# Two transformer blocks over eight batches: a work order of its own for each engine, a fetch in two parts, and stack loads of 256 KB

## What is computed

```python
xn = _layernorm(x)
x = x + _L0_attn_ref(xn, ...) + _L0_ffn_ref(xn, ...)     # block 0
xn = _layernorm(x)
x = x + _L1_attn_ref(xn, ...) + _L1_ffn_ref(xn, ...)     # block 1
```

## Time and profile before

| | us |
|---|---|
| median of 3 runs | 795.38 |
| lowest and highest | 793.43, 795.67 |
| the profiled execution, whole | 790.95 |
| its span | 789.2 |

### The profile page before, as it was taken

The page is one execution under the profiler, slowest core; times in us unless marked ns, Lnnn a source line. Parts: engine busy times, 40 slices in busy tenths (PEclk is TensorE's granted clock), DMA queues, the critical chain, the costliest instruction groups (busy, mean ns, idle before and its releaser), DMA issues. The chain is left out here.

```text
span 789.2 us, 19922 instructions
## 1 busy us (share of the span) xinstructions
PE 654.3 (83%) x6455; PEld 481.4 (61%) x6455; DVE 568.9 (72%) x2201; ACT 465.8 (59%) x1223; POOL 267.8 (34%) x386
## 2 busy tenths in 40 slices
PE   0466677999699997999799997999699997899834
PEld 0344455777477765777577765777477776677512
DVE  3679877786579757786679757786679768776464
ACT  2458765955388445955388445955388447944433
POOL 7926441233213331223213331323213332134334
PEclk9969797999999998999999998999989999999969
DMA  7643021301211031301211031301211030300552
GB/s 219 231 132 99 23 72 50 105 19 55 84 54 55 15 109 29 108 15 55 83 54 55 15 109 29 108 15 55 83 54 55 15 108 15 108 2 15 165 182 69
DMA packets 49580, 57.69 MB, mean 73 GB/s; under 512 B 5056, under 2 KB 40000, under 8 KB 49472
## 3 DMA queue, kind: packets, MB, share of 16 engines
q1 hardware_dynamic: 46432, 52.44, 20.8%
q0 software_dynamic: 1056, 2.62, 1.0%
q10 hardware_dynamic: 1984, 1.21, 0.6%
HBM read 33.71 MB, written 22.54 MB: 71 GB/s over the span
## 5 line engine op out<-in xcount | busy, mean ns | idle before, releaser
L1001 ACT ACTIVATE probs<-probs,nmax 128x256 f32<-128x256 f32 (+1 forms) x256 | 113.5, 446 | 51.4 <-DVE nmax L1511 50.5
L844 POOL TENSOR_TENSOR h_lo<-hid,h_hi 128x512 f16<-128x512 f32 x64 | 74.2, 1160 | 203.5 <-ACT h_hi L982 203.3
L1125 PE MATMUL gen_ps<-xe_hi,gu_hi 128*128 128x256 f16 x512 | 101.6, 281 | 3.2 <-DVE gated L1457 2.0
L1125 PE MATMUL gen_ps<-xe_lo,gu_hi 128*128 128x256 f16 x512 | 100.7, 279 | 0.0
L1125 PE MATMUL gen_ps<-xe_hi,gu_lo 128*128 128x256 f16 x512 | 100.4, 279 | 0.0
L1029 ACT ACTIVATE et<-turn_ps 128x384 f32<-128x384 f32 x128 | 55.7, 489 | 66.1 <-PE turn_ps L1215 56.1
L1511 DVE CUSTOM_DVE_ANT_0 probs<-score_ps,bias 128x256 f32<-128x256 f32 (+1 forms) x256 | 80.2, 352 | 19.0 <-PE score_ps L1182 11.2
L1525 DVE CUSTOM_DVE_ANT_0 junk<-score_ps,bias 128x256 bf16<-128x256 f32 (+1 forms) x256 | 76.0, 352 | 16.2 <-PE score_ps L1182 11.3
L1180 PE MATMUL score_ps<-k_stack,q_stack 64*128 64x256 f16 x256 | 37.9, 292 | 51.5 <-DVE nmax L1511 17.9
L1536 DVE TENSOR_SCALAR probs<-probs,rsum 128x256 f32<-128x256 f32 (+1 forms) x256 | 74.6, 334 | 4.5
L1473 DVE SCALAR_TENSOR_TENSOR acc<-gen_ps,w,acc 128x256 f32<-128x256 f32 x112 | 48.8, 477 | 25.5 <-PE gen_ps L1136 25.4
(11 more groups left out here) (210 smaller groups left out, 1664.5 us busy)
## 6 DMA issues: line engine op xcount, KB each, us to landing
scr_q<-parts SPq DMA_DIRECT2D x32, 256.0 KB, 2.7
scr_k<-parts SPq DMA_DIRECT2D x32, 256.0 KB, 3.0
q_stack<-scr_q SPq DMA_DIRECT2D x64, 128.0 KB, 3.0
k_stack<-scr_k SPq DMA_DIRECT2D x64, 128.0 KB, 3.1
x<-in_x SPq DMA_DIRECT2D x8, 256.0 KB, 3.5
y_dram<-yx_sb SPq DMA_DIRECT2D x7, 256.0 KB, 2.2
x_dram<-yx_sb SPq DMA_DIRECT2D x7, 256.0 KB, 2.3
gu_hi<-y_dram SPq DMA_DIRECT2D x1, 1792.0 KB, 7.7
```

The costliest lines, as they stand in the source:

```text
L844: pool.tensor_tensor(h0_lo[:, e], hid0[:, e], h0_hi[:, e], ALU.subtract).then_inc(s_h0l, 1)
L1001: last = act.activation(probs[:, k, lo:hi], probs[:, k, lo:hi], ACT.Exp, scale=-1.0, bias=nmax[:, k, j:j + 1], accum_out=esum[:, k, j:j + 1])
L1125: last = pe.matmul(g[:, S * f:S * f + S], w[:, st.arg, m, k, cols], xx[:, k, :], start=(i == 0), stop=(i == len(terms) - 1))
```

## The change

- The texts, `with_heads` and `LAG` go. In their place stands `ORDER_TEXT`, with a list of single steps for each of PE, ACT, DVE and POOL in each pass; each engine's list holds only the steps in which it has work. SP goes on taking PE's list.
- `load_stack` issues one load of 256 KB (128 rows) for q and one for k, in place of two of 128 KB each; PE's wait counts 32 for a stack, not 64.
- `fetch` has two parts: part 0 brings batches 0 to 5 and waits for the stores of these only, part 1 brings batch 6 and waits for its store. ACT and POOL wait for part 0 at `quant:0` and for part 1 at `quant:6`. In SP's list part 1 stands behind the output stores of `quant:0` and `quant:1`.
- The first reduction of `qmax` (over the y maxima) becomes a step of its own, `ymx`.

The number of compute instructions of each kind, their shapes and the semaphores are otherwise the same.

```diff
-                for hp in range(2):
-                    four = slice(8 * u + 4 * hp, 8 * u + 4 * hp + 4)
-                    for src, dst in zip(scr[l], (q_stack, k_stack)):
-                        sp.dma_start(dst[l][u][KR * hp:KR * hp + KR],
-                                     src.rearrange("s (c h) n -> (s c) h n", h=H)[:, four, :]).then_inc(s_stack[l][u], 16)
+                for src, dst in zip(scr[l], (q_stack, k_stack)):
+                    by_head = src.rearrange("s (c u p i) n -> u p (s c) (i n)", u=2, p=2, i=H // 4)
+                    sp.dma_start(dst[l][u][:].rearrange("r i n -> r (i n)"), by_head[u]).then_inc(s_stack[l][u], 16)
...
+                    c = st.arg
                     sp.wait_ge(s_acc, NT * ACC_STEPS * B)
-                    sp.wait_ge(s_yw, 16 * B)
-                    sp.wait_ge(s_x2w, 16 * B)
-                    done = NT * (B - 1)
-                    sp.dma_start(y_all[:, 0:done, :], y_tiles[:, 0:done, :]).then_inc(s_fin, 16)
-                    sp.dma_start(x_all[:, 0:done, :], x2_tiles[:, 0:done, :]).then_inc(s_fin, 16)
+                    sp.wait_ge(s_yw, 16 * (EARLY + 1 if c == 0 else B))
+                    sp.wait_ge(s_x2w, 16 * (EARLY + 1 if c == 0 else B))
+                    part = slice(0, NT * EARLY) if c == 0 else slice(NT * EARLY, NT * (B - 1))
+                    sp.dma_start(y_all[:, part, :], y_tiles[:, part, :]).then_inc(s_fin[c], 16)
+                    sp.dma_start(x_all[:, part, :], x2_tiles[:, part, :]).then_inc(s_fin[c], 16)
...
-                    if c == 0:
-                        pool.wait_ge(s_fin, 32)
+                    if c in (0, EARLY):
+                        pool.wait_ge(s_fin[c // EARLY], 32)
```

More of the change, by code:

```diff
@@ L128, in in_turn @@
     return [next(turns[key(item)[0]]) for item in items]
[L131 to L137, removed]
-            out.append(("score", s, 0))
-        if 0 <= s - NORM_LAG < H:
-            out.append(("norm", s - NORM_LAG, 0))
-        t = s - TURN_LAG
-        if 0 <= t < H:
-            out.append(("turn", t, 0))
-        t -= VALUE_LAG
-        if 0 <= t < H and t % G4 == G4 - 1:
-            out.append(("value", t // G4, 0))
-    for item in order:
-        if isinstance(item, int):
-            head(item)
-        else:
-            out.append(item)
-    return out
@@ L156 @@
-FIRST_ORDER = """
-    ln0a setup:0 ln0b split:0 split:3 tr0 setup:2 xe split:2 vsplit:0 split:1 v0:0 q0 k0 gate:0 setup:1 l0 split:5 rt1
-    v0:1 split:4 up:0 gate:1 0 rt2 split:7 1 up:1 split:6 down:0 2 gate:2 3 down:1 4 up:2 split:8 gate:3 5 split:9
-    up:3 down:2 tern:0 split:10 6 tmx:0 tern:1 gate:4 7 down:3 8 split:11 9 up:4 10 11 12 gate:5 tern:3 down:4 13
-    tern:2 split:13 +ln0a tern:4 up:5 tsm:0 tern:6 split:12 tern:5 gate:6 14 gate:7 +ln0b up:6 down:5 15 16 tmx:1 up:7
-    vsplit:1 +tr0 17 down:6 tern:8 tern:7 +q0 +k0 tern:9 +v0:0 +l0 18 19 +v0:1 down:7 op0 +xe tsm:1 tern:10 tern:11
@@ L162 @@
-"""
-STEADY_ORDER = """
-    0 1 ln1a gate:0 2 ln1b up:0 rt1 tr1 3 rt2 4 q1 k1 5 gate:1 down:0 6 up:1 gate:2 w1:3 w1:0 l1 w1:2 w1:1 v1 7 8 h1:0
-    up:2 9 gate:3 10 h1:1 down:1 11 h1:2 b:1 h1:3 up:3 12 down:2 13 14 down:3 15 b:0 16 gate:4 17 b:3 mp:0 up:4 +ln0a
-    mp:1 18 b:2 w2 b:4 19 m:0 gate:5 s:1 b:5 down:4 +ln0b op0 s:0 b:6 +tr0 up:5 b:7 s:2 gate:6 +q0 +k0 s:3 y:0 +l0
-    up:6 m:1 gate:7 s:4 y:1 s:5 up:7 down:5 s:6 y:2 s:7 +v0:0 down:6 y:3 down:7 +v0:1 op1 +xe
-"""
-LAST_ORDER = """
-    ln1a 0 gate:0 ln1b rt1 rt2 1 tr1 2 gate:1 up:0 3 q1 k1 4 down:0 5 up:1 6 gate:2 v1 h1:1 w1:2 w1:1 w1:0 l1 w1:3
-    up:2 7 8 down:1 9 gate:3 10 down:2 11 12 h1:3 h1:0 13 b:0 up:3 14 15 h1:2 b:1 gate:4 16 up:4 b:4 17 18 gate:5 b:3
-    down:4 mp:0 19 b:2 m:0 up:5 down:3 b:5 gate:6 up:6 gate:7 up:7 s:2 b:6 down:5 op0 s:0 mp:1 b:7 down:7 down:6 s:1
-    +ln1a y:0 s:3 m:1 +ln1b w2 +tr1 s:4 y:1 +q1 +l1 +k1 s:5 s:6 y:2 s:7 +w1:0 +w1:2 y:3 +w1:1 +w1:3 op1
@@ L182, in order_of @@
+BLOCK1 = {"b", "mp", "m", "s", "y", "ln1a", "ln1b", "tr1", "q1", "k1", "l1", "v1", "w1", "h1", "w2", "op1", "ymx", "qmax", "quant", "fetch"}
 def order_of(text):
@@ L204, in uses @@
     return sum(s[0] in BANKED for s in order)
-ORDERS = {"first": order_of(FIRST_ORDER), "steady": order_of(STEADY_ORDER),
-          "last": order_of(LAST_ORDER), "final": order_of(FINAL_ORDER)}
+ORDER_OF = {engine: {kind: order_of(text) for kind, text in kinds.items()} for engine, kinds in ORDER_TEXT.items()}
+ORDERS = ORDER_OF["tensor"]
 USES_STEADY = uses(ORDERS["steady"])
@@ L217 @@
 ACC_STEPS = E + 1
+EARLY = B - 2
 class Index:
@@ L290, in stages @@
         out.append(st)
-    def behind(st):
-        for key in (f"{kind}.{st.name}:{st.arg}", f"{kind}.{st.name}", f"{st.name}:{st.arg}", st.name):
-            if key in lag:
-                return lag[key]
-        return 0
-    late = [i + behind(st) for i, st in enumerate(out)]
-    return in_turn([out[i] for i in sorted(range(len(out)), key=lambda i: (late[i], i))],
-                   lambda st: (st.name, st.n.off, st.arg))
+    if engine not in ORDER_OF:
+        return out
+    by_step = dict(zip(ORDERS[kind], out))
+    return [by_step[step] for step in ORDER_OF[engine][kind]]
 def last_users(kind, it):
@@ L306, in last_users @@
     if kind != "first":
-        stages("last" if kind == "final" else "steady", it.plus(-1), {}, users)
+        stages("last" if kind == "final" else "steady", it.plus(-1), "", users)
     return users
@@ L331, in settle, with run_passes @@
     eng.sem_inc(passed, 1)
-def run_passes(eng, do, before_block1, lag):
-    for st in stages("first", Index(None, 0), lag):
+def run_passes(eng, do, before_block1, engine):
+    for st in stages("first", Index(None, 0), engine):
         do(st)
@@ L339, in run_passes @@
     with eng.Fori(0, STEADY) as j:
-        for st in stages("steady", Index(j, 1), lag):
+        for st in stages("steady", Index(j, 1), engine):
             do(st)
-    for st in stages("last", Index(None, B - 1), lag):
+    for st in stages("last", Index(None, B - 1), engine):
         do(st)
-    for st in stages("final", Index(None, B), lag):
+    for st in stages("final", Index(None, B), engine):
         do(st)
@@ L720, in _ @@
             load_raw(1)
-            for st in stages("first", Index(None, 0), {}):
+            for st in stages("first", Index(None, 0), "sync"):
                 if st.name == "ln0a" and st.n.off == 1:
@@ L729, in _ @@
                 load_x(it.plus(1))
-                for st in stages("steady", it, {}):
+                for st in stages("steady", it, "sync"):
                     do(st)
-            for st in stages("last", Index(None, B - 1), {}):
+            for st in stages("last", Index(None, B - 1), "sync"):
                 do(st)
-            for st in stages("final", Index(None, B), {}):
+            for st in stages("final", Index(None, B), "sync"):
                 do(st)
```

149 lines of the change are left out of this document (126 added, 23 removed), and 41 rows, old and new, of the table LAG.

## The result

The changed kernel takes 863.86 us (median of 4 runs, 863.63 to 864.01), the kernel before 795.52 (4 runs). The ratio is 1.0864, 95% interval 1.0845 to 1.0884: slower by 8.6%, where I had forecast 782.8 us. The profiled execution has a span of 862.0 us, against 789.2.

The account below looks back on a forecast made before the run. PE was taken to bound the steady iteration, DVE to be nearest full in the first pass, the end to be a chain. Gains 3.7 + 4.5 + 0 + 4.4 = 12.6 us from the 795.38 median gave 782.8 us, range 771 to 794.

Parts of the forecast that it names:

- the landing of the 256 KB load: First pass: a merged load lands in 3.2 us, and two fewer issues bring the first score 1.2 us earlier.
- In the steady passes the stacks are loaded several us before they are used, so there the saving is 0.: Steady iterations: the merged loads save 0; if the cover went, at most 1.2 us for a stack.
- The queue: SP, first pass: eight issues of about 0.60 us each; halving them brings the weight loads behind them 2.4 us earlier.
- late next: Final pass: the scale, at about 756.5, holds quant:0, which starts 2.1 us earlier, not 3.6.
- First pass: First pass: l0 1.3 us earlier from the lists, 2.4 from fewer issues; 3.7 us carried to its end.
- Steady: Six steady iterations: q1 starts 0.75 us earlier in each by the new order, 4.5 us in all.
- my fourth case: Rival, chance 0.11: without the wait at tr1 the clock holds, 3.1 us more in some four iterations, 770.4 us.
- an iteration is over 89 us: Steady loop: sign that the forecast is wrong; iterations of 87.7 us were expected against 88.5.
- Last pass: Last pass, up to op1 of batch 6: gain 0, between 1.5 us either way.
- Final pass: Final pass: 4.4 us gained from the split fetch and new order, bounds 1 and 6.
- Part (c): Final pass order: fewer quants ahead of s:0, b:6 and b:7 bring ACT's s:3 4.4 us earlier.
- The slow rival: Steady iterations, chance 0.11: the half-speed clock stretch of 6.3 us doubles, costing 3.15 us an iteration, 801.7 us.

Follow-up runs that it names:

- the kernel with two loads: Changed kernel with the stack loads as before, two of 128 KB for q and two for k: 776.59 us, ratio 0.9784; run again 779.21 us, 0.9849.
- The four passes timed alone: Old loads, new lists in one pass only (the final one with the split fetch), against the kernel before: ratios first 0.9907, steady 0.9857, last 0.9970, final 0.9952.

## Why the prediction was wrong

**The step that failed: the landing of the 256 KB load.** I bounded it "between the 3.0 us of 128 KB and that plus the transfer of another 128 KB", 0.4 us by the rate of the fetch, and took 3.2. The stack is whole 12.7 us behind its first issue, where it took 5.2 before and where I counted on 4.0 (1.2 less). The error isn't in the number but in what I scaled: bytes, at a rate that the fetch had on all engines. I had the diff with `u p (s c) (i n)` before me and read it only for which bytes it brings. The shape was a fact of the change, and neither my bounds nor a rival had it. It was also the one change in my sum for which no row of before stood. What the runs showed in its place: the load runs on 2 engines, not 16, and brings some 50 GB/s where the old loads brought 199.

**"In the steady passes the stacks are loaded several us before they are used, so there the saving is 0."** This was wrong for the kernel before too. At `b:0` PE takes its first score 5.4 us behind the first issue, and a stack takes 5.2: the cover is 0.2 us, if the 5.2 of the first pass hold here. I bounded what is lost if that cover goes with the same 1.2 us for a stack, a bound for a saving, not for a loss. It became a wait of 7.3 to 8.0 us in each iteration, 45.4 in six. Against the same lists with loads on all engines (520.9 us) the six iterations are 53.6 us longer; 4.7 of the other 8.2 are a wait at a first score, and for the rest I can name the lower clock but haven't measured it apart. Had I looked up who uses the stack and when, I'd have seen that a longer load would be paid in full, six times.

**The queue.** I counted what an issue costs SP (0.60 us) as fixed. With a narrow load it is 0.5 to 8.1 us. It looks as if SP stands at the issue until loads ahead have drained; what it stands for the profile doesn't show. All that is queued on SP behind it comes late too: the weight loads, the store of x, the fetch. That is how the end lost 16.0 us, where I had a gain of 4.4. The scale, "late next" in my text, was ready at 823.6, 6 us before the fetch. My 10.7 us for part 0 (12.49 x 6/7) took the queue ahead of it as free; the part took 17.82.

**The list terms.** In the kernel with two loads they can be held against my steps.
- First pass: l0 at 25.6 us against 26.5 walked, score:0 at 37.49 with both loads still there, where I had 37.8 with the merged one. The pass gives 4.7 us, not 1.3 without the loads. My walk on ACT was right to within 1 us; the 2.83 us that I left for l0 was 1.22, and I didn't follow what DVE and the splits gain behind l0.
- Steady: the gain is 8.6 us, not 4.5, and only a third of it came as I had it. Cut at the loop's first matmul on PE, the four iterations between the loop's turns take 87.8 us with the new lists and 88.5 with the old ones (means of four kernels each): 0.7 an iteration, where I had 0.75. But that is 2.8 us and not 4.5; the other 5.8 lie at the two ends of the loop, 3.1 in the first iteration and 2.7 in the sixth up to op1. I had nothing for them, and no run shows which step gives them. The sum of all six came out above my 4.5 with a step that was worth 2.8; that the pass gained at least what I forecast is luck in part.
- What I walked inside an iteration holds, counted from the loop's first matmul: q1 starts 9.6 to 10.3 us behind it (I had 10.2; before 10.3 to 11.0), and the wait at score:2 is 1.5 us in most iterations and up to 2.5. What I left out is that the first matmul itself moves. At the loop's turn PE idles for 1.7 to 2.4 us in the kernel before; with the new steady lists it idles for 3.2 to 3.6 in 13 of 20 turns (with the old ones in 2 of 20), and the profile names no releaser. That is why iterations seem to be of two kinds when they are cut at SP's load of x. Two that follow each other, in the kernel with the steady lists alone:

```profile
297.00:386.10 89.10, 80.57 (x810) 59.94 (x811) 65.11 (x268) 53.78 (x148) 25.61 (x41) 0.96 0.18 58
386.10:471.40 85.30, 78.24 (x805) 59.05 (x802) 65.00 (x268) 53.80 (x148) 25.68 (x41) 0.98 0.19 61
```

From first matmul to first matmul the same two take 87.5 and 86.9 us (PE's timeline):

```profile
298.23 0.60 PE L1138 MATMUL gen_ps<-xe_hi,gu_hi 128*128 128x256 f16 x2 [3.35 <-issue]
...
385.71 0.39 PE L1138 MATMUL gen_ps<-xe_hi,gu_hi 128*128 128x256 f16 x2 [1.71 <-issue]
...
472.63 0.61 PE L1138 MATMUL gen_ps<-xe_hi,gu_hi 128*128 128x256 f16 x2 [3.32 <-issue]
```

So these rows don't show my fourth case, the clock that holds. The kernel before has a granted clock of 0.98 in its second iteration too, and that one takes 88.5 us. And my sign of being wrong, "an iteration is over 89 us", was met here without the merged load.
- Last pass: 0 taken, 3.8 us measured, outside my 1.5 either way; but some 3 us of it are paid back in the final pass through the later w2 (46.8 us with all new lists, 43.8 with those of the final pass alone).
- Final pass: with its lists alone, quant:0 starts 14.1 us behind op1, released by the scale, as I had it ("14 us behind the last op1"). Part (c) was too large: the first exponential behind y:0 comes 25.6 us behind op1, 2.9 us sooner and not 4.4, and from quant:0 to the end it is 29.7 us and not 28.3.

The slow rival that I had named (the clock, 801.7) points to the right side for another reason, and didn't come. Without the merged load the result lies inside my range of 771 to 794 (776.6 and 779.2), but not by my terms: I had 10.2 us for lists and fetch, and the two kernels gave 17.2 and 12.0.

**What stays open.** The four passes timed alone add up to 25 us by the ratios (20 in the traces), all together gave 12 to 17. The last and the final pass explain some 3 us of this, the rest lies within the intervals. Where the 5.8 us at the ends of the loop come from, why PE idles longer at the loop's turn, and what SP waits for at a long issue, no run shows.

## What to carry to other kernels

When a change merges or reshapes a DMA, write down the sizes of the issued source and destination from the outermost dimension on, before any thought of bytes: here one of 64 rows that became 2 x 64 took more than twice as long until the same bytes were in. For every transfer that the change touches, look up in the trace of before who waits for it and with how much cover, and let the bound for a loss come from there. Here the DMA that got slower also delayed what stood behind it on its queue. And where a loop is judged by its iterations, cut them at the engine that bounds the loop, since another engine's mark can move against it by 2 us.

## What the runs showed of the hardware

- A stack of 512 KB arrived in 5.2 us on 16 engines, 9.4 on four and 13.7 on two. While the loads of the changed kernel ran, the DMAs moved 51 GB/s at a share of 0.13, about two engines, so some 25 KB in a us for one (an estimate). From four to two engines each has 128 KB more and the time grows by 4.3 us, which would be 30.
- SP's issue of a DMA isn't of fixed cost. The issue of a k load took 0.49 us at best and 8.10 at worst in the changed kernel (timeline of SP, first iteration), 0.58 to 1.19 with two loads on all engines:

```profile
218.48 8.10 SPq L689 DMA_DIRECT2D k_stack<-scr_k  x1
```

- Half as many stack loads of 256 KB, on all engines, gave PE nothing: one landed after 5.0 us, one of 128 KB after 3.0.
